# Turning the second half of the activations by 32x32 squares and a way through memory, in a fused attention and feed-forward kernel

## The reference

```
x = x + layernorm(attention(layernorm(x)))
x = x + layernorm(ffn(layernorm(x)))

attention(h): qkv = silu(h @ qkv_w.T), 32 heads of 128
              linear attention with decay, carried as a 128x128 state from block to block
              out = (sigmoid(h @ gate_w.T) * norm_w * rms_normalise(attn)) @ out_w.T
ffn(h):       (silu(h @ gate.T) * (h @ up.T)) @ down.T, ternary weights with scales
```

## Time and profile before

| | |
|---|---|
| median of 3 runs | 2402.28 us (2402.16 to 2402.33) |
| profiled execution | 2404.0 us, span 2402.0 us |
| TensorE matmuls busy | 2354.1 us, 98% |
| DVE busy | 1391.3 us, 58% |
| ScalarE busy | 1207.0 us, 50% |
| POOL busy | 1679.4 us, 70% |
| granted TensorE clock, mean | 0.996 |

### The profile page before, as it was taken

One profiled execution on the slowest core, in us unless ns is written; L12 is line 12 of the kernel. 1 busy time (PEld: TensorE's weight loads), 2 busy tenths in 40 slices (PEclk: granted clock), 3 DMA queues, 4 the chain that ended last, 5 costly groups with the idle time before them and its releaser, 6 DMA issues.

```text
span 2402.0 us, 38322 instructions
## 1 busy us (share of the span) xinstructions
PE 2354.1 (98%) x12276; PEld 2003.5 (83%) x12276; DVE 1391.3 (58%) x2475; ACT 1207.0 (50%) x1748; POOL 1679.4 (70%) x1322
## 2 busy tenths in 40 slices
PE   7999999999999999999999999999999999899997
PEld 6788888888888888878888888888888888788886
DVE  5556656555666666656555555555555555555655
ACT  5555555554444444435454455544444444366563
POOL 4777777777777777756777777777777776474675
PEclk9999999999999999999999999999999999999999
DMA  4434444444444444554444333443333334512212
GB/s 136 127 127 142 133 128 128 136 142 142 141 139 128 134 141 142 167 186 145 141 140 131 129 125 131 130 140 128 119 118 110 109 107 143 181 57 76 80 62 97
DMA packets 165953, 307.15 MB, mean 128 GB/s; under 512 B 22384, under 2 KB 102256, under 8 KB 163184
## 3 DMA queue, kind: packets, MB, share of 16 engines
q1 hardware_dynamic: 138992, 269.93, 34.4%
q10 hardware_dynamic: 26880, 36.18, 4.6%
HBM read 219.02 MB, written 87.03 MB: 127 GB/s over the span
## 4 chain that ended last, share of the span: by engine, by line
PE 87%; ACT 3%; DMA 3%; issue 3%; DVE 3%; POOL 1%; SPq 0%; DVEq 0%; ACTq 0%; POOLq 0%
PE proj L2003 53%; PE yp L2003 18%; PE sc L2050 5%; PE sc L2073 4%; PE sc L2076 4%; PE sc L2063 3%; DMA k_blocks<-pd 1%; DVE pd L1507 1%; ACT piece L1015 0%; ACT k L923 0%; ACT L923 0%; ACT sq L937 0%; DMA fs_stage<-ffn_scales 0%; DMA k_tok<-k_blocks 0%; DMA y<-x 0%
## 5 line engine op out<-in xcount | busy, mean ns | idle before, releaser
L2003 PE MATMUL proj<-xb,w_odd 128*128 128x512 f32 x2694 | 704.7, 399 | 7.1 <-DVE g L1470 2.1
L2003 PE MATMUL proj<-xb,w_even 128*128 128x512 f32 x2694 | 679.9, 396 | 7.6 <-DVE xb L1422 3.6
L2003 PEld LDWEIGHTS proj<-xb,w_even 128*128 128x128 f32 x2694 | 498.1, 189 | 109.9 <-issue 5.0
L2003 PEld LDWEIGHTS proj<-xb,w_odd 128*128 128x128 f32 x2694 | 489.1, 189 | 106.6 <-DVE q L1478 5.4
L607 POOL TENSOR_TENSOR qd<-q,table 128x512 f32<-128x512 f32 x128 | 164.0, 1294 | 191.5 <-ACT q L923 191.5
L1552 DVE TENSOR_TENSOR g<-sc,g 128x512 f32<-128x512 f32 x128 | 88.5, 691 | 297.1 <-ACT sq L937 296.9
L598 POOL TENSOR_TENSOR ow_lo<-v_tok,ow_hi 128x1024 fp32r<-128x1024 f32 x32 | 76.6, 2394 | 231.2 <-ACT ow_hi L891 231.2
L1559 DVE TENSOR_TENSOR y<-yp,y 128x512 f32<-128x512 f32 x240 | 164.5, 685 | 124.1 <-PE yp L2003 123.1
L2003 PE MATMUL proj<-x_t,f_hi 128*128 128x512 f32 x896 | 214.2, 392 | 3.2 <-issue 3.2
L2003 PE MATMUL yp<-ow_hi,g_hi 128*128 128x512 f32 x512 | 202.4, 395 | 1.4 <-DVE y L1559 1.4
L592 POOL TENSOR_TENSOR w_odd<-ws,w_odd 128x1024 fp32r<-128x1024 f32 x63 | 151.3, 2402 | 73.0 <-ACT w_odd L885 73.0
(11 more groups left out here) (194 smaller groups left out, 4417.5 us busy)
## 6 DMA issues: line engine op xcount, KB each, us to landing
raw<-w_attn SPq DMA_DIRECT2D x128, 512.0 KB, 3.6
k_blocks<-pd SPq DMA_DIRECT2D x64, 512.0 KB, 3.4
k_tok<-k_blocks SPq DMA_DIRECT2D x256, 128.0 KB, 2.8
v_blocks<-vf SPq DMA_DIRECT2D x64, 512.0 KB, 2.7
v_tok<-v_blocks SPq DMA_DIRECT2D x252, 128.0 KB, 2.8
v_tok<-w_out SPq DMA_DIRECT2D x32, 512.0 KB, 4.4
fraw<-w_ints SPq DMA_DIRECT2D x13, 1024.0 KB, 4.9
piece<-w_ints ACTq DMA_DIRECT2D x21, 512.0 KB, 4.3
```

Of the source, the lines that this page charges most:

```text
L2003: last = pe.matmul(psum, s, m, start=start and n == 0, stop=n == len(terms) - 1, skip_group_check=more)
```

## The change

Piece j is no longer transposed by TensorE. DVE transposes it in squares of 32 into columns 1024 to 1535 of `piece` (`turn_piece`, two instructions, after keep_s3 of QQ). SP writes the 256 KB to a DRAM tensor `p_blocks` (after k_read(w, 1)) and reads them back with the squares in their places (four DMAs, after k_read(w, 0)) into the first 512 columns. ScalarE's `keep_piece` copies from there and stands, together with `piece_high`, after gated_hi(a, 1, 1); DVE's `mix_piece` stands after finish_22 of VV. `project_out` no longer waits for the piece. TensorE's windows 2 to 14 become one loop; DVE's and SP's loops are cut where the piece's half, or the piece itself, changes.

```diff
+            def piece_there(j):
+                sp.wait_ge(piece_turned, 2 * (j + 1))
+                sp.dma_start(p_blocks.rearrange("i d b n -> (i d) (b n)"),
+                             piece[:, 2 * HID:3 * HID]).then_inc(piece_out, 16)
+
+            def piece_back_in(j):
+                sp.wait_ge(piece_out, 16 * (j + 1))
+                for b in range(QUADS):
+                    sp.dma_start(piece_t[quad(b)].rearrange("d (i n) -> d i n", i=QUADS),
+                                 p_blocks[:, :, b].rearrange("i d n -> d i n")).then_inc(piece_back, 16)
...
                 k_write(w, 1)
                 k_read(w, 1)
+                if piece_way:
+                    piece_there(a)
                 k_write(w, 0)
                 k_read(w, 0)
+                if piece_way:
+                    piece_back_in(a)
...
             def keep_piece(j):
-                act.wait_ge(piece_turned, j + 1)
-                wait(act, piece_lo_out, 16 * j)
+                act.wait_ge(piece_back, 16 * QUADS * (j + 1))
                 for m in range(2):
-                    act.activation(mix[:, B_21 * m:B_21 * m + T_3 + 1:T_3],
-                                   yp[0][:, 2 * P * m:2 * P * (m + 1)].rearrange("p (s n) -> p s n", s=HALVES),
+                    act.activation(mix[:, B_21 * m:B_21 * m + T_3 + 1:T_3]
+                                   .rearrange("p s (i t) -> p s i t", i=QUADS),
+                                   piece_t.rearrange("p (i m s t) -> p m s i t", i=QUADS, m=2, s=HALVES)[:, m],
                                    ACT.Copy).then_inc(piece_kept, 1)
...
                 gated_hi(a, 0, 1)
-                if part is not None:
-                    keep_piece(part)
...
                 square(a, 1, 1)
-                if part is not None:
-                    piece_high(part)
                 activate(w, VV, OUT11)
                 gated_hi(a, 1, 0)
                 gated_hi(a, 1, 1)
                 if part is not None:
+                    keep_piece(part)
+                    piece_high(part)
                     store_high(part)
...
+            def turn_piece(j, i):
+                dve.wait_ge(piece_normed, 2 * (j + 1))
+                for m in range(2):
+                    dve.transpose(piece_quads[:, :, m],
+                                  tiles[:, :, chunk(2 * m + i)].rearrange("p s (b t) -> p b s t", b=QUADS))\
+                        .then_inc(piece_turned, 1)
...
                 keep_s3(w, QQ)
+                if part is not None:
+                    turn_piece(part, part_half)
                 turn_k(w, 0, 0)
...
                 finish_21(w, QQ)
-                if part is not None:
-                    mix_piece(part)
                 gate(a, 1, 0)
...
                 finish_22(w, VV)
+                if part is not None:
+                    mix_piece(part)
                 finish_12(w, VV)
...
-                    if part is not None:
-                        pe.wait_ge(piece_kept, 2 * (a + 1))
...
-            def turn_piece(a, i, j):
-                pe.wait_ge(piece_normed, 2 * (j + 1))
-                wait(pe, yacc_done, BT * a - 1)
-                for m in range(2):
-                    for s in range(HALVES):
-                        last = pe.transpose(yp[0][:, chunk(2 * m + s)], tiles[:, s, chunk(2 * m + i)],
-                                            ident[:, :])
-                last.then_inc(piece_turned, 1)
...
                 attend(a, 0, 1)
-                if part is not None:
-                    turn_piece(a, part, a)
                 product(w, QQ, 7)
```

More of the change, by code:

```diff
@@ L182, in sandwich_kernel @@
         piece_normed, piece_turned, piece_kept = sem("piece_normed"), sem("piece_turned"), sem("piece_kept")
+        piece_out, piece_back = sem("piece_out"), sem("piece_back")
         piece_mixed, piece_hi_done, piece_lo_done = sem("piece_mixed"), sem("piece_hi_done"), sem("piece_lo_done")
@@ L276, in sandwich_kernel @@
         v_tok_apart = piece[:, 0:2 * HID].rearrange("p (i h c d) -> p i h c d", i=QUADS, h=2, c=CH)
+        piece_quads = piece[:, 2 * HID:3 * HID].rearrange("p (b m s t) -> p b m s t", b=QUADS, m=2, s=HALVES)
+        piece_t = piece[:, 0:HID]
         kt = pd[:, 0].rearrange("p h c n -> p (h c n)").rearrange("p (b h c d) -> p b h c d",
@@ L317, in sandwich_kernel @@
         v_blocks = nc.dram_tensor("v_blocks", (HALVES, QUADS, QUAD, QUADS, 2 * CH * QUAD), F32).ap()
+        p_blocks = nc.dram_tensor("p_blocks", (QUADS, QUAD, QUADS, HID // QUADS), F32).ap()
         x_blocks = nc.dram_tensor("x_blocks", (NB, P, 2, RT, SEG), F32).ap()
@@ L436, in ffn_activations, with window @@
                     .then_inc(x_t_in[s], 16)
-            def window(w, pair, next_weights=True, second_batch=False, out_first=False):
+            def window(w, pair, next_weights=True, second_batch=False, out_first=False, piece_way=False):
                 a = w - 1
@@ L504, in _ @@
             first_window()
-            window(1, 1)
-            with sp.Fori(2, PAIRS - 1) as w:
+            window(1, 1, piece_way=True)
+            with sp.Fori(2, 2 * CH + 1) as w:
+                window(w, w, piece_way=True)
+            with sp.Fori(2 * CH + 1, PAIRS - 1) as w:
                 window(w, w)
@@ L1645, in window @@
             def window(w, first=False, checks=None, rms_of=None, ends_first=False, finish=None, begin=None,
-                       part=None, next_part=False, v_second=v_tok):
+                       part=None, part_half=0, next_part=False, v_second=v_tok):
                 a = w - 1
@@ L1781, in _ @@
             window(1, first=True, part=0, next_part=True)
-            with dve.Fori(2, 2 * CH) as w:
+            with dve.Fori(2, CH + 1) as w:
                 window(w, part=w - 1, next_part=True)
-            window(2 * CH, part=2 * CH - 1)
+            with dve.Fori(CH + 1, 2 * CH) as w:
+                window(w, part=w - 1, part_half=1, next_part=True)
+            window(2 * CH, part=2 * CH - 1, part_half=1)
             with dve.Fori(2 * CH + 1, PAIRS - 1) as w:
@@ L2078, in attend, with project_out @@
                 last.then_inc(attn_done, 1)
-            def project_out(a, t, tile=None, downs=0, part=None):
+            def project_out(a, t, tile=None, downs=0):
                 if t == 0:
@@ L2172, in turn_tile, with window @@
                 last.then_inc(tile_turned, 1)
-            def turn_piece(a, i, j):
-                pe.wait_ge(piece_normed, 2 * (j + 1))
-                wait(pe, yacc_done, BT * a - 1)
-                for m in range(2):
-                    for s in range(HALVES):
-                        last = pe.transpose(yp[0][:, chunk(2 * m + s)], tiles[:, s, chunk(2 * m + i)],
-                                            ident[:, :])
-                last.then_inc(piece_turned, 1)
-            def window(w, x_wait=False, rms_of=None, tile=None, part=None):
+            def window(w, x_wait=False, rms_of=None, tile=None):
                 a = w - 1
@@ L2213, in window @@
                     pe.wait_ge(rms_ready, rms_of + 1)
-                project_out(a, 0, tile, part=part)
+                project_out(a, 0, tile)
                 product(w, QQ, 4)
@@ L2251, in _ @@
             first_window()
[L2252 to L2257, removed]
+            window(1)
+            with pe.Fori(2, PAIRS - 1) as w:
                 window(w)
```

## The result

The changed kernel takes 2413.44 us (median of 7 runs, 2411.29 to 2418.78) beside 2402.56 us of the kernel before on the same chip (7 runs, 2402.16 to 2406.85): a ratio of 1.0043, 95% interval [1.0034, 1.0053]. It is slower by more than what can be told from no change. The profiled execution took 2411.3 us with a span of 2409.2 us, against 2404.0 and 2402.0 us: +7.2 us, somewhat less than the medians' distance, since it is the quickest of the seven.

The account below looks back on a forecast made before the run. The prediction took ScalarE, DVE and the k DMA to set the pace up to (QQ, 4), not TensorE. Terms of 0 plus 5.2 us for the mix, less about 0.5 for window 9, on 2402.28 gave 2407.0; range 2399 to 2414.

Parts of the forecast that it names:

- TensorE's removal: Windows 1 to 8: 0.93 us a window taken off TensorE is waited away at (QQ, 3); 0 us, bounds 0 to 7.4 gain.
- Rival B: TensorE paces the chain up to (QQ, 4) after all: 3.1 to 7.4 us faster, 2395 to 2399; chance 0.10.
- The prediction's sign for it: TensorE's weight loads: the wait before (QQ, 3) at 1.2 to 1.4 us in windows 2 to 8; still 0.35 would mean B.
- DVE's transposes and SP's way: DVE's two transposes (0.7 to 0.8 us) hidden in its idle 1.80 us, SP's write and four reads hidden too; 0 us.
- The mix: DVE's four operations behind finish_22(VV), blocked by POOL, delay finish_12: half of eight windows at 1.3 us, +5.2, bounds 0 to 12.4.
- Rival A: The mix slips between POOL's instructions by pairs, done by 186.7 in every window: 2402.3 us, within 1.5; chance 0.27.
- the price at (GG, 7): TensorE's product (GG, 7) needs finish_12(VV), queued behind the late mix: 0 to 1.55 us late a window.
- the one that the prediction dismissed in one sentence: ScalarE late by 1 to 2 us reaches v and the next window's keep_s3 of k, absorbed by TensorE's 1.3 us wait.
- The wait before (QQ, 4): TensorE's wait for DVE's finish_22 in windows 2 to 8, 0.46 us in window 2, stays as before.
- Window 9: TensorE's 1.46 us wait there, behind the longest L1567, may not come again: about 0.5 us taken off.
- Rival D: The longer wait at (QQ, 3) costs TensorE its clock, 13.6 us less the 0.46 wait: about 2412; chance 0.05.
- Rival C: The mix is blocked until POOL runs dry in all windows: 12.4 us slower, 2414.7; chance 0.10.

Follow-up runs that it names:

- fourth experiment: The kernel before without TensorE's transposes of the pieces, keep_piece copying the tiles as they are: 2401.99 us, ratio 0.9999.
- fifth: The kernel before with ScalarE's square root for the piece moved ahead of activate(KK, OUT11) and DVE's scales_of_piece behind keep_s3(KK): 2392.42 us, ratio 0.9961.
- third experiment: The changed kernel without SP's write to and reads from p_blocks, keep_piece copying the normalised tiles: 2415.97 us, ratio 1.0058 to the kernel before.
- first experiment: The changed kernel with the mix's four subtractions replaced by one-input 128x128 transposes: 2405.73 us, ratio 1.0017 to the kernel before.
- second experiment: The kernel before with only mix_piece moved behind finish_22(VV) and piece_high behind gated_hi(1, 1): 2410.69 us, ratio 1.0037.
- tenth: The kernel before with the piece's square root and scales moved early and without TensorE's transposes of the piece: 2386.65 us, ratio 0.9943.

## Why the prediction was right, and where not

**TensorE's removal, booked at 0: right, and for the reason given.** The chain from keep_s1(QQ) to (QQ, 3) kept its 15.17 us, the fourth experiment put the removal alone at 0.9999, and shortening the chain (fifth) gave 0.0039. Rival B is refuted. The prediction's sign for it, 1.2 to 1.4 us before (QQ, 3) in every window, came out as 0.69 there and 0.71 at (KK, 3): the sum is right, the split was not foreseen, since I had no reason for k to be late. One reading was a little too smooth: ScalarE isn't busy without a gap from 148.31 to 159.32, it waits 0.85 us for DVE's gate at 157.00. That gap belongs to the same chain and changes nothing in the argument.

**DVE's transposes and SP's way, booked at 0: right.** 0.76 us for the two, as the upper estimate said, inside DVE's idle time, of which 1.36 us are left. The p_blocks write took its slot ahead of the k write, and the third experiment got nothing back from removing it. A few us for all of the new steps together are not excluded: with the mix's second input gone, the first experiment still lies 0.0017 (4 us) above the kernel before.

**The mix, booked at +5.2 us: the cause right, the size on the low side, the place wrong.** By the runs the late mix costs more than the 5.2: 6 to 7 us (first experiment against the changed kernel) or 8 to 9 us (second experiment, the move alone). The contention is there in every window, 1.37 us for an operation of 0.28, and the two-input form is its condition (first experiment). Rival A, the mix slipping in by pairs, is refuted. But the step of the prediction that put the price at (GG, 7) failed. The mix began at 313.76, 16.2 us behind (QQ, 4), just where the prediction put its start, but its first two operations got in at two of POOL's short instructions and cost 1.14 us together, so it ended at 317.57 and finish_12 at 318.18, 20.6 us behind (QQ, 4), just ahead of the 20.85 at which TensorE wants (GG, 7). I had let the four go at four ends of gated lows and decays, over a us apart, and took an earlier start among the shorter instructions ahead of 183.5 for the exception; it was the rule in windows 2 to 8.

The price came by the other way, the one that the prediction dismissed in one sentence: "that reaches v and, in the next window, k's keep_s3, after (QQ, 1) has gone, where TensorE now has 1.3 us of wait to absorb it". keep_s3 of k, and its wait at (KK, 3), does fall into that slack and is free. But keep_s2 of k stands ahead of it in the same queue on DVE, and its product, (KK, 5), comes ahead of (QQ, 1) on TensorE; there is no slack there. 4.8 us in four of seven windows, 1.2 us each, is close to the forecast's "half of the windows at 1.3", but at another place and by another path, so the closeness is luck. Shown by the second experiment, which has the moves alone, and by the first, which takes the contention out and (KK, 5)'s wait with it.

**The wait before (QQ, 4), forecast "as before": off by +2.5 us.** 0.2 us a window, since the k DMA that finish_22 stands behind lands so much later (2.72 us behind keep_s3's start instead of 2.49). The added traffic isn't the reason: without it (third experiment) (QQ, 4) waits nearly as long, 5.9 us in 7 times against 6.2. 1.4 us of it is one wait of 1.9 us in window 2. Waits of 1.3 and 1.1 us stand at the same product and window in the fourth and tenth experiments, which have no transposes of the piece on DVE and nothing new on SP; what they share with the changed kernel is that TensorE's transposes are gone. Why it is late there is not known.

**Window 9.** Its wait is gone as half expected: 1.5 us, where the sum took 0.5.

**The clock.** Rival D did not come: 0.996.

**Rival C** gave 2414.7, nearer to the median than the forecast is, but by another mechanism: it needs the mix blocked until POOL runs dry and paid at (GG, 7), which didn't wait in any window from 2 to 8 of the changed kernel.

By rows the sum is 4.8 at (KK, 5), 2.5 at (QQ, 4), 1.2 more of waiting at (KK, 3) and (QQ, 3) than what TensorE was spared, and -1.5 for window 9: 7.0, where the span grew by 7.2. That agreement is partly luck. By the starts of keep_s1(QQ), the changed kernel reaches window 1 1.4 us earlier (81.67 against 83.07), takes 6.7 us more for windows 1 to 9, 2.7 more from window 16 to 17, and 0.9 less for all the rest: the step at window 16, which the prediction didn't book and no experiment explains, is hidden by gains elsewhere. The medians lie 10.9 us apart; the rest is between executions, and the profiled one doesn't show it.

## What to carry to other kernels

When a step is made late, follow it through every queue until it reaches the busiest engine, and look up for each instruction queued behind the late one whether its consumer stands ahead of the start of the chain that sets the pace or behind it: the same lateness was free at (KK, 3) and paid at (KK, 5), 3.3 us apart. Work taken off the busiest engine pays only after the chain that it waits for has been shortened: the transposes were worth nothing until two calls were moved, and those two calls were worth about 9 us by themselves. An activation function of another table in a chain costs two loads around it, 2.76 us here for 0.20 us of work, and moving it pays only where its input is already there.

## What the runs showed of the hardware

- A DVE subtraction with two SBUF inputs beside a POOL stream without gaps takes about the time of the POOL instruction that it runs beside (0.77 or 1.38 us in place of 0.28), one per POOL instruction as a rule, and ends 0.15 us behind the end of that instruction. Several such ends can be missed: of the maxima L1567, with 128x1 inputs, each ends within 0.02 us of the end of a POOL instruction, and the one of 4.78 us (640.94 to 645.72) let four such ends pass. Transposes with one input, in the mix's places, take 0.27 to 0.31 us.
- The same four operations take 0.46 us each on POOL itself, 1.8 us of its time against 3.8 us of DVE's.
- Two DVE transposes of 128x256 with strided squares of 32 took 0.42 us each, where one of 128x512 takes 0.71.
- Four reads of 128 KB, the last of them issued behind the first of two loads of 256 KB, landed up to 5.3 us after their issue instead of 2.6 to 2.9, and the loads took 4.5 to 5.4 us instead of 3.0 to 3.1.
